# A perceiver block with a mixture of experts: down gather round eight PSUM banks, one loop over the down tiles, last down logits inside the first down steps

## Chip, core and metric

One core of one Trainium2 chip. The metric is the device time of one execution in microseconds (us), the median over several executions. Inputs and outputs are float32.

## The reference, cut to what matters

```python
x = x + cross_attention(layernorm(x), ctx)      # (32, 64, 512) queries, 1601 context rows each
x = x + causal_attention(layernorm(x))          # 16 heads
x = x + ffn(layernorm(x))

def kmoe(x_flat, W_router, A, B, scale, bias, d_in1, d_in2, d_out1, d_out2, top_k):
    logits = x_flat @ W_router.T                # 64 experts
    vals, idx = jax.lax.top_k(logits, 2)
    probs = jax.nn.softmax(vals, axis=-1)
    xs = x_flat.reshape(-1, d_in1, d_in2)
    Y = jnp.einsum('nkoi,nij,nkpj->nkop', A[idx], xs, B[idx])
    out = jnp.einsum('nkop,nk->nop', Y, probs)
    return out.reshape(-1, d_out1 * d_out2) * scale + bias

def ffn(x):                                     # rows of 1024: two tokens together, 1024 rows in all
    h = kmoe(x.reshape(-1, 1024), W_up, A_up, B_up, ..., 32, 32, 64, 64, 2)
    h = jax.nn.gelu(h, approximate=False)       # rows of 4096
    return kmoe(h, W_down, A_down, B_down, ..., 64, 64, 32, 32, 2)
```

## The kernel before

Everything that changes lies in `mixture`, the last of the stages: the feed-forward part with its two layers, "up" and "down". The 1024 rows are worked on in `T_N` = 4 tiles of 256 rows. Each engine runs its own block of instructions, and counting semaphores order them. VectorE (DVE), ScalarE (ACT), GpSimd (POOL) and SyncE (SP, which issues the DMAs) have straight code for all tiles; TensorE (`@block.tensor`) has loops on the chip (`pe.Fori`) and branches (`pe.If`), since its code is long: each float32 matmul of the program is recorded as two matmuls and two weight loads (a transpose as one of each).

A tile of the up layer on TensorE: `gather_up` in 8 rounds takes each row's factors out of the expert tables by a matmul with a one-hot matrix; `rows` transposes the next tile's rows; `logits_dn` forms the router logits of the down layer of the tile before (128 matmuls), `logits_up` those of the next tile, `fold_dn` adds two halves of the down logits; `steps_up` runs 16 steps in pairs: `first_up` twice (L1642), `second_up` twice (L1659). ScalarE copies the result of a first product out of PSUM (`mid_out`, L1515), stages input (`stage_x`), and applies gelu (`gelu`, L1520) to what VectorE wrote in `bias` (L1332). GpSimd stages the factors (`stage_a`, `stage_b`). In ScalarE's order each step n has: `mid_out(n)`, `stage_x(n+2)`, `gelu(n-2)`. The tile's hidden values go out to HBM by DMA.

After the last up tile come the down tiles. `gather_dn` (L1680) has two tables v = 0 and 1, and 8 units g in each; a unit is 8 matmuls (16 recorded) into two PSUM banks. Table 0 uses banks 0 to 3 and table 1 banks 4 to 7, so unit g waits until unit g-2 of its table has been copied out (`gather_out_dn`, VectorE L1342, ScalarE L1527). `BY_ACT` says which units ScalarE copies: 5 of the first 8 and 6 of the second. Then `steps_dn` runs 16 steps: `first_dn` (L1693, 32 matmuls, 64 recorded) into banks 0 to 3, `mid_out`, `second_dn` (L1708, 16 matmuls, 32 recorded) into bank 4 or 5, `y_out` (VectorE L1355). `steps_dn` is two first products, a loop of 7 rounds (second, first, second, first), and two second products. `stage_h` (VectorE, L1349), `stage_a_dn` (ScalarE, L1533) and `stage_b_dn` (GpSimd, L1215) feed it; `stage_b_dn` of step 0 waits for all evictions of table 1. `results_back` (VectorE transposes, L1362) and `residual` (L1368) finish a tile while the next is worked on. SyncE loads the hidden values of a tile (`load_h`, 4 transfers of 1 MB) and the residual input (`load_x2`, 2 of 512 KB).

What stands between: behind the first down gather TensorE runs the last tile's `logits_dn` (L1598) into banks 0 and 1, VectorE copies them out (`part`, L1449), TensorE folds them (L1605), VectorE copies the logits, and only then `steps_dn(0)` begins. `load_h(1)` waits for these logits. The choice of experts that they give (`greatest` to `weigh`) is made by VectorE beside the steps of down tile 0 and transposed behind them (`transpose_choices`, L1612). The loop over down tiles covers tiles 0 to 2, each with the gather of the next tile at its end; the last `steps_dn` stands after the loop as a second copy of the code:

```python
            gather_dn(0)
            all_units(pe, 0, 0)
            pe.wait_ge(s_gelu, T_N * STEPS)
            logits_dn()
            ...
            with pe.Fori(0, T_N - 1) as T:
                steps_dn(T)
                ...
                gather_dn(T + 1)
            steps_dn(T_N - 1)
```

Code of an engine comes from HBM by DMA. In the trace TensorE's arrives in pieces of 16 KB on the queue q8, the other engines' in pieces of 8 KB on q14.

## Time and profile before

| | us |
|---|---|
| median of 3 runs | 1546.29 |
| lowest, highest | 1537.84, 1546.94 |
| the profiled execution, its own time | 1545.56 |
| its span | 1543.6 |
| mean granted TensorE clock in it | 0.932 |
| TensorE busy (88% of the span) | 1363.7 |
| VectorE, ScalarE, GpSimd busy | 815.6, 443.3, 207.0 |

The profile is one execution. Times in its rows are microseconds from the start of the span, durations of one instruction nanoseconds. PE is TensorE's matmul side and PEld its weight loads, PEldq its sequencer. "Clock" is the share of TensorE's full clock of 2.4 GHz that was granted: 1.00, or 0.50, which is 1.2 GHz. "Issue" is time in which an engine waited for no other engine and no transfer that the profile knows.

### The profile page before, as it was taken

How to read it: one execution, taken by the hardware profiler on the slowest of the kernel's cores; microseconds unless marked ns; L12 is line 12 of the kernel's file. 1: busy time of each engine (PE TensorE's matmuls, PEld its weight loads, DVE VectorE, ACT ScalarE, POOL GpSimd, SP SyncE). 2: the span in 40 equal slices, each digit the busy share in tenths (PEclk: the TensorE clock that was granted, in tenths of full speed). 3: DMA queues.
4: the chain of work that ended last, by engine and by line, in shares of the span. 5: the costliest groups of instructions: out<-in, count | busy, mean ns of one | idle time of the engine just before them, and what ended most of it. 6: DMA issues, size and time to landing. Idle time of an engine off the chain costs nothing.

```text
span 1543.6 us, 70151 instructions
## 1 busy us (share of the span) xinstructions
PE 1363.7 (88%) x32072; PEld 931.8 (60%) x32072; DVE 815.6 (53%) x1511; ACT 443.3 (29%) x887; POOL 207.0 (13%) x361
## 2 busy tenths in 40 slices
PE   7896899999999999799999999867888888798887
PEld 4895454444444444366666666556677676677666
DVE  1224666566667665135655566443645645246645
ACT  0230211121112111122212122124544535336653
POOL 0000000000000000011111111113341432113211
PEclk9898899999999999999999999977999999769995
DMA  4575387687868885521111100130212206324102
GB/s 191 169 206 199 109 288 242 207 276 269 275 212 293 284 275 204 118 47 55 54 54 54 49 32 14 56 110 29 109 55 82 108 0 244 141 81 160 58 1 82
DMA packets 57230, 212.00 MB, mean 137 GB/s; under 512 B 11760, under 2 KB 28144, under 8 KB 42640
## 3 DMA queue, kind: packets, MB, share of 16 engines
q1 hardware_dynamic: 57104, 210.14, 39.8%
q8 instruction: 100, 1.64, 0.4%
q14 instruction: 26, 0.21, 0.0%
HBM read 172.37 MB, written 37.75 MB: 136 GB/s over the span
## 4 chain that ended last, share of the span: by engine, by line
PE 41%; DVE 5%; issue 5%; ACT 5%; POOL 2%; DMA 0%; DVEq 0%; POOLq 0%; SPq 0%; ACTq 0%
PE ps L895 8%; PE ps L1693 5%; PE ps L1627 4%; PE ps L886 4%; PE ps L996 4%; PE ps L1680 3%; PE ps L1642 2%; PE ps L1708 2%; PE ps L1598 2%; PE ps L916 2%; PE ps L1659 2%; ACT arena L1527 1%; PE ps L1589 1%; PE ps L906 1%; PE ps L938 1%
## 5 line engine op out<-in xcount | busy, mean ns | idle before, releaser
L476 DVE STREAM_TRANSPOSE arena<-arena 128x384 f32<-128x384 f32 (+1 forms) x512 | 276.7, 587 | 133.3 <-PE ps L563 132.4
L563 PE MATMUL ps<-arena 32*64 32x224 f32 (+3 forms) x8192 | 241.4, 348 | 28.4 <-issue 20.0
L563 PEld LDWEIGHTS ps<-arena 32*64 32x64 f32 x8192 | 160.5, 134 | 140.7 <-DVE arena L476 87.1
L587 PE MATMUL ps<-arena 128*64 128x512 f32 (+1 forms) x832 | 209.7, 615 | 0.1
L1515 ACT COPY arena<-ps 128x512 f32<-128x512 f32 x128 | 75.0, 586 | 167.6 <-PE ps L1642 86.2
L895 PE MATMUL ps<-arena 128*128 128x256 f32 x512 | 116.6, 387 | 6.3 <-ACT arena L847 6.3
L895 PEld LDWEIGHTS ps<-arena 128*128 128x128 f32 x512 | 97.3, 193 | 21.8 <-ACT arena L847 7.2
L534 ACT ACTIVATE arena<-ps,arena 128x416 f32<-128x416 f32 (+2 forms) x80 | 41.1, 531 | 229.9 <-DVE arena L488 229.9
L1693 PE MATMUL ps<-arena 64*64 64x32 f32 x4096 | 95.2, 250 | 10.0 <-issue 6.5
L587 PEld LDWEIGHTS ps<-arena 128*64 128x64 f32 (+1 forms) x832 | 49.5, 136 | 87.1 <-issue 87.1
L1693 PEld LDWEIGHTS ps<-arena 64*64 64x64 f32 x4096 | 88.7, 170 | 14.3 <-issue 10.9
L1332 DVE SCALAR_TENSOR_TENSOR arena<-ps,arena 128x512 f32<-128x512 f32 x64 | 69.3, 1110 | 49.0 <-PE ps L1659 49.0
L1627 PE MATMUL ps<-arena 64*32 64x128 f32 x4096 | 71.1, 277 | 14.9 <-issue 6.5
L1680 PE MATMUL ps<-arena 64*64 64x256 f32 x1024 | 70.0, 404 | 11.5 <-ACT arena L1527 5.0
L1627 PEld LDWEIGHTS ps<-arena 64*32 64x32 f32 x4096 | 59.5, 107 | 26.5 <-issue 22.7
L721 POOL MEMSET arena<- 128x128 f32 x1 | 0.2, 206 | 537.3 <-POOLq L432 537.3
L886 PE MATMUL ps<-arena 128*128 128x512 f32 x128 | 61.9, 620 | 8.2 <-ACT arena L876 4.8
L1642 PE MATMUL ps<-arena 32*32 32x64 f32 x4096 | 57.0, 233 | 13.4 <-issue 6.1
L1215 POOL COPY arena<-arena 128x512 f32<-128x512 f32 x64 | 40.9, 642 | 194.9 <-ACT arena L1527 99.6
L1680 PEld LDWEIGHTS ps<-arena 64*64 64x64 f32 x1024 | 42.8, 139 | 37.8 <-issue 30.9
L1642 PEld LDWEIGHTS ps<-arena 32*32 32x32 f32 x4096 | 47.9, 108 | 21.4 <-issue 21.0
L313 PE MATMUL ps<-arena 128*128 128x256 f32 x256 | 60.4, 395 | 0.0
(136 smaller groups left out, 1850.8 us busy)
## 6 DMA issues: line engine op xcount, KB each, us to landing
arena<-ctx SPq DMA_DIRECT2D x32, 1792.0 KB
arena<-ctx SPq DMA_DIRECT2D x32, 1280.0 KB
arena<-q_n SPq DMA_DIRECT2D x64, 256.0 KB, 13.9
h_n<-arena SPq DMA_DIRECT2D x16, 1024.0 KB, 4.5
arena<-h_n SPq DMA_DIRECT2D x16, 1024.0 KB, 8.3
arena<-x SPq DMA_DIRECT2D x16, 512.0 KB, 4.3
x_n<-arena SPq DMA_DIRECT2D x16, 512.0 KB, 3.1
arena<-x_n SPq DMA_DIRECT2D x16, 512.0 KB, 4.1
```

The costliest lines, as they stand in the source:

```text
L476: vec.transpose(z[:, at % RING, :, 0:nt * 32].rearrange("p b (j t) -> p b j t", t=32), slots[slot_of(k)][:, :, 0:nt, db * 32:(db + 1) * 32 ...
L563: last = pe.matmul(ps[b * SEQ:(b + 1) * SEQ, tb, g * 224:g * 224 + w], qs[p % 2][r, db, b * SEQ:(b + 1) * SEQ], z[r, at % RING, b, 0:w], s ...
L587: last = pe.matmul(ps[b * SEQ:(b + 1) * SEQ, OB, :], probt[0:r, j, b * SEQ:(b + 1) * SEQ], slot[0:r, b, jj, :], start=j == 0, stop=j == TI ...
L886: x = pe.matmul(ps[:, par, :], ats[:, c, par::2], w["xwv"][:, c, :], start=c == 0, stop=c == DC - 1)
L895: last = pe.matmul(ps[:, bank, m % 2 * QROWS:(m % 2 + 1) * QROWS], w[n][:, c, m * P:(m + 1) * P], lnt[:, c, :], start=c == 0, stop=c == DC ...
L996: last = pe.matmul(ps[:, 4 + par, :], aot[:, c, par::2], w["swo"][:, c, :], start=c == 0, stop=c == DC - 1)
L1332: vec.scalar_tensor_tensor(h[:, q, :, at].rearrange("p j g -> p g j"), ps[:, b:b + 2, :].rearrange("p b (g x) -> p (b g) x", x=2 * F1)[:, ...
L1515: act.copy(mid[u].rearrange("p (b x) -> p b x", b=2), ps[:, 2 * u:2 * u + 2, 0:256]).then_inc(s_me, 1)
L1627: last = pe.matmul(ps[c * R:(c + 1) * R, 4 * v + hf, o * P:(o + 1) * P], tab_st[v][r, o, :], x, start=True, stop=True)
L1642: last = pe.matmul(ps[q * R:(q + 1) * R, 2 * u + c // 2, m * F1:(m + 1) * F1], xs[rows_c, m, :], four(st_a[u])[rows_c, m // 2 * 2 + k, m % ...
L1680: last = pe.matmul(ps[t * E:(t + 1) * E, 4 * v + 2 * (g % 2) + hf, o % 2 * 2 * P:(o % 2 + 1) * 2 * P], tab_dn[v][r, o, :], x, start=True, ...
L1693: last = pe.matmul(ps[k * F1:(k + 1) * F1, 2 * u + t, g * D1:(g + 1) * D1], st_h[u][rows_t, g * F1:(g + 1) * F1], two(st_a[u])[rows_t, k, ...
```

## The change

- `gather_dn` goes round all eight banks: unit g of either table uses banks 2(g mod 4) and the next. A unit waits for the eviction of the fourth unit before it (`unit_out`), unit 2 of table 0 also for the last `y_out`; `steps_dn` waits for units 4 and 5 of table 1 before its two first products. `BY_ACT` gives ScalarE 4 and 5 units.
- The loop of TensorE over the down tiles covers all four; behind the last steps a branch skips the gather.
- `logits_dn` and `fold_dn` of the last tile move into rounds 0 and 2 of the step loop of tile 0, with banks 6 and 7, behind the branch `i < 3`; VectorE's copies and the choices move into steps 2 to 14. `exponential` on GpSimd moves from step 6 to 10, `next_choices` from 8 to 4.
- VectorE stages the first two steps and transposes results earlier in the gather.
- SyncE loads x2 of tile 0 after the logits. `y`, `yt` and `x2b` change places in SBUF.
- In the up layer ScalarE does the two `mid_out` and `stage_x` of a pair of steps, then its two gelus.

```diff
@@ -1025,8 +1025,8 @@
     wr_dn = wr_at.rearrange("p (o e) -> p o e", e=E)
-    y, yt = wr_at[:, 0:2 * D * 2].rearrange("p (t r b) -> p t r b", t=2, r=R), wr_at[:, 4 * D:8 * D].rearrange("p (t f) -> p t f", t=2)
-    x2b = tables["up_at"].rearrange("p (t f) -> p t f", t=2)
+    y = tables["up_at"].rearrange("p (t r b) -> p t r b", t=2, r=R)
+    x2b, yt = (wr_at[:, u * 4 * D:(u + 1) * 4 * D].rearrange("p (t f) -> p t f", t=2) for u in range(2))
     st_a, st_b, st_h = ([area(512) for _ in range(2)] for _ in range(3))
...
     hb_at = top_area.at
@@ -1055,7 +1055,7 @@
-    BY_ACT = ((0, 2, 4, 6, 7), (0, 2, 4, 5, 6, 7))
+    BY_ACT = ((0, 2, 4, 6), (0, 2, 4, 6, 7))
...
     s_wr, s_x2, s_end, s_hd = sem("mo_wr"), sem("mo_x2"), sem("mo_end"), sem("mo_hd")
@@ -1091,7 +1091,7 @@
         dst = fac[v].rearrange("p (m o f) -> p m o f", o=D1 // 2, f=2)[:, :, 2 * g:2 * g + 2, :]
-        b = 4 * v + 2 * (g % 2)
+        b = 2 * (g % 4)
         return dst, ps[:, b:b + 2, :].rearrange("p f (o m) -> p m o f", o=2)
...
     def unit_done(v, g, T):
@@ -1158,10 +1158,9 @@
                 load_h(0, q)
-            sp.wait_ge(s_ts, 16 * T_N)
-            load_x2(0)
             sp.wait_ge(s_hd, 16 * 4 * T_N)
             sp.wait_ge(s_lgd, T_N)
+            load_x2(0)
             for q in range(4):
...
             for T in range(T_N):
@@ -1245,19 +1244,23 @@
                     stage_b_dn(T, n)
-                    if T == 0 and n == 6:
+                    if T == 0 and n == 10:
                         exponential("dn", T_N - 1)
-                    if T + 1 < T_N and n == 8:
+                    if T + 1 < T_N and n == 4:
                         next_choices(T + 1)
...
         def _(vec):
-            def logits(k, i):
+            def parts(count, bank):
+                vec.wait_ge(s_lgd, count)
+                vec.tensor_copy(part, ps[:, bank:bank + 2, 0:P]).then_inc(s_part, 1)
+
+            def logits(k, i, bank):
                 if k == "up":
...
                     vec.wait_ge(s_lgb, i + 1)
-                vec.tensor_copy(lg[k], ps[:, 4 if k == "up" else 5, 0:2 * E].rearrange("p (t e) -> p t e", t=2)).then_inc(s_lge, 1)
+                vec.tensor_copy(lg[k], ps[:, bank, 0:2 * E].rearrange("p (t e) -> p t e", t=2)).then_inc(s_lge, 1)
...
                 vec.wait_ge(s_lge, choice(k, i)[1])
@@ -1375,7 +1378,7 @@
             vec.sem_inc(s_ohe["dn"][1], CREDIT)
-            logits("up", 0)
+            logits("up", 0, 4)
             greatest("up", 0)
...
             index("up", 0, 0)
@@ -1393,14 +1396,13 @@
                 if T:
-                    vec.wait_ge(s_lgd, T)
-                    vec.tensor_copy(part, ps[:, 0:2, 0:P]).then_inc(s_part, 1)
+                    parts(T, 0)
                 if T + 1 < T_N:
-                    logits("up", T + 1)
+                    logits("up", T + 1, 4)
                 else:
...
                 if T:
-                    logits("dn", T - 1)
+                    logits("dn", T - 1, 5)
                 for n in range(STEPS):
...
                     if T + 1 < T_N:
@@ -1442,16 +1444,11 @@
                             gather_out_dn(T, v, g)
-                        if v == 0 and g == 7 and T:
-                            results_back(T - 1, 0)
-                if T == 0:
-                    vec.wait_ge(s_lgd, T_N)
-                    vec.tensor_copy(part, ps[:, 0:2, 0:P]).then_inc(s_part, 1)
-                    logits("dn", T_N - 1)
-                stage_h(T, 0)
-                stage_h(T, 1)
-                if T:
-                    results_back(T - 1, 1)
+                        if v == 0 and g in (3, 7) and T:
+                            results_back(T - 1, g // 7)
+                        if v == 1 and g == 1:
+                            stage_h(T, 0)
+                            stage_h(T, 1)
                 for n in range(STEPS):
...
                         stage_h(T, n + 2)
@@ -1459,18 +1456,22 @@
                     if T == 0:
-                        if n == 1:
+                        if n == 2:
+                            parts(T_N, 6)
+                        if n == 6:
+                            logits("dn", T_N - 1, 6)
+                        if n == 7:
                             greatest("dn", T_N - 1)
                             difference("dn", T_N - 1)
-                        if n == 2:
+                        if n == 8:
                             index("dn", T_N - 1, 0)
...
                             index_out("dn", T_N - 1)
-                        if n == 4:
+                        if n == 9:
                             one_hot("dn", T_N - 1)
-                        if n == 10:
+                        if n == 13:
                             weights_of("dn", T_N - 1)
-                        if n == 11:
+                        if n == 14:
                             weigh("dn", T_N - 1)
...
                     one_hot_out("dn", T_N - 1, 7)
@@ -1546,12 +1547,14 @@
                     rows_out(T + 1)
-                for n in range(STEPS):
-                    mid_out(STEPS * T + n)
-                    if n + 2 < STEPS:
-                        stage_x(T, n + 2)
-                    if n >= 2:
-                        gelu(T, n - 2)
+                for n in range(0, STEPS, 2):
+                    for b in range(2):
+                        mid_out(STEPS * T + n + b)
+                        if n + 2 < STEPS:
+                            stage_x(T, n + b + 2)
+                    for b in range(2):
+                        if n >= 2:
+                            gelu(T, n + b - 2)
                 gelu(T, STEPS - 2)
...
                     one_hot_out("up", T + 1, 2)
@@ -1590,19 +1593,19 @@
-            def logits_dn():
+            def logits_dn(bank):
                 for p in range(F1):
...
                         half = p % 2
-                        last = pe.matmul(ps[half * E:(half + 1) * E, t, 0:P], wr_dn[r, p, :], h[r, :, p, :],
+                        last = pe.matmul(ps[half * E:(half + 1) * E, bank + t, 0:P], wr_dn[r, p, :], h[r, :, p, :],
                                          start=p < 2, stop=p >= F1 - 2)
...
-            def fold_dn(count):
+            def fold_dn(count, bank):
                 pe.wait_ge(s_part, count)
                 for t in range(2):
-                    last = pe.matmul(ps[:, 5, t * E:(t + 1) * E], part[:, t, :], fold, start=True, stop=True)
+                    last = pe.matmul(ps[:, bank, t * E:(t + 1) * E], part[:, t, :], fold, start=True, stop=True)
                 last.then_inc(s_lgb, 1)
...
             def transpose_choices(k, bank, count):
@@ -1661,23 +1664,28 @@
+            def unit_out(v, g, T):
+
+                done, first = unit_done(v, g, 0)
+                pe.wait_ge(done, T * (len(BY_ACT[v]) if g in BY_ACT[v] else 8 - len(BY_ACT[v])) + first)
+                apart(pe, SPARE)
+
...
                 for v in range(2):
-                    if v == 1:
-                        pe.wait_ge(s_ye, T * STEPS + CREDIT)
                     apart(pe, SPARE)
                     for g in range(8):
-                        if g >= 2:
-                            done, count = unit_done(v, g - 2, 0)
-                            pe.wait_ge(done, T * (len(BY_ACT[v]) if g - 2 in BY_ACT[v] else 8 - len(BY_ACT[v])) + count)
+                        if v == 0 and g == 2:
+                            pe.wait_ge(s_ye, T * STEPS + CREDIT)
                             apart(pe, SPARE)
+                        if v or g >= 4:
+                            unit_out(*divmod(8 * v + g - 4, 8), T)
                         for o in range(2 * g, 2 * g + 2):
...
                                     x = ohx_d[r, 0, 2 * t:2 * t + 2, :].rearrange("p k n -> p (k n)") if v == 0 else ohx_k[r, t]
-                                    last = pe.matmul(ps[t * E:(t + 1) * E, 4 * v + 2 * (g % 2) + hf, o % 2 * 2 * P:(o % 2 + 1) * 2 * P],
+                                    last = pe.matmul(ps[t * E:(t + 1) * E, 2 * (g % 4) + hf, o % 2 * 2 * P:(o % 2 + 1) * 2 * P],
                                                      tab_dn[v][r, o, :], x, start=True, stop=True)
@@ -1718,13 +1726,21 @@
             def steps_dn(T):
+                unit_out(1, 4, T)
                 first_dn(T * STEPS, 0)
+                unit_out(1, 5, T)
                 first_dn(T * STEPS + 1, 1)
...
                     first_dn(i * 2 + 3, 1)
+                    with pe.If(i < 3):
+                        with pe.If(i < 1):
+                            pe.wait_ge(s_gelu, T_N * STEPS)
+                            logits_dn(6)
+                        with pe.If(i > 1):
+                            fold_dn(T_N, 6)
                 second_dn(T * STEPS + STEPS - 2, 0)
@@ -1751,11 +1767,11 @@
                     apart(pe, SPARE)
-                    logits_dn()
+                    logits_dn(0)
                 with pe.If(T < T_N - 1):
...
                 with pe.If(T > 0):
-                    fold_dn(T)
+                    fold_dn(T, 5)
                 pe.wait_ge(s_lge, T * 2 + 2)
...
                 steps_up(T)
@@ -1768,21 +1784,16 @@
             gather_dn(0)
-            all_units(pe, 0, 0)
-            pe.wait_ge(s_gelu, T_N * STEPS)
-            logits_dn()
-            all_units(pe, 1, 0)
-            fold_dn(T_N)
-            pe.wait_ge(s_lge, 9)
-            with pe.Fori(0, T_N - 1) as T:
+            with pe.Fori(0, T_N) as T:
                 steps_dn(T)
                 with pe.If(T < 1):
+                    pe.wait_ge(s_lge, 9)
                     transpose_choices("dn", 6, T_N)
...
                         pe.wait_ge(s_ohe["dn"][e], 4 + CREDIT)
-                pe.wait_ge(s_oc, T * 2 + 2)
-                gather_dn(T + 1)
-            steps_dn(T_N - 1)
+                with pe.If(T < T_N - 1):
+                    pe.wait_ge(s_oc, T * 2 + 2)
+                    gather_dn(T + 1)
...
 _IN = ["x", "ctx", "wq", "wk", "bq", "bk", "bv", "xwv", "swq", "swk", "swv", "swo", "bo", "db",
```

## Rows read from the trace of the kernel before

**Rows 1.** The page, part 2: granted TensorE clock in 40 slices of the span.
```profile
PEclk9898899999999999999999999977999999769995
```

**Rows 2.** Windows: stretch, length, busy time (count) by engine, clock, DMA share, GB/s.
```profile
1296.00:1316.50 20.50, 17.43 (x256) 11.61 (x260) 6.12 (x5) 11.04 (x12) 0.00 (x0) 0.92 0.77 300
1316.50:1327.60 11.10, 8.55 (x267) 7.70 (x257) 1.43 (x4) 1.01 (x1) 1.17 (x2) 1.00 0.12 27
1327.60:1373.10 45.50, 38.44 (x1537) 36.11 (x1537) 17.84 (x43) 16.63 (x30) 11.21 (x17) 0.57 0.45 180
1376.10:1399.10 23.00, 20.98 (x384) 13.42 (x384) 11.85 (x10) 13.21 (x16) 1.11 (x2) 0.89 0.01 2
1399.10:1425.70 26.60, 22.89 (x1408) 20.98 (x1408) 17.14 (x30) 15.39 (x28) 10.74 (x17) 1.00 0.52 198
1425.70:1447.10 21.40, 18.71 (x389) 12.21 (x392) 12.13 (x11) 13.34 (x16) 1.22 (x2) 1.00 0.11 47
1447.10:1473.90 26.80, 22.98 (x1408) 21.21 (x1408) 17.04 (x31) 15.24 (x28) 10.77 (x17) 1.00 0.20 79
1473.90:1496.00 22.10, 18.51 (x384) 12.12 (x384) 12.11 (x11) 14.06 (x17) 1.50 (x2) 1.00 0.00 1
1496.00:1533.70 37.70, 34.67 (x1408) 32.20 (x1408) 17.33 (x30) 14.44 (x26) 8.62 (x14) 0.56 0.15 57
1376.10:1381.40 5.30, 5.25 (x52) 3.16 (x53) 1.22 (x1) 1.02 (x1) 0.00 (x0) 0.50 0.00 0
1118.40:1125.60 7.20, 7.20 (x257) 7.03 (x256) 0.00 (x0) 0.87 (x2) 0.00 (x0) 1.00 0.00 0
```

**Rows 3.** The chain that ended last, in tile 0's steps: start, us, what.
```profile
1330.73 3.91 issue
...
1338.34 2.60 issue
```

**Rows 4.** Timeline around the stalls of tile 0 and of the last tile.
```profile
1334.64 1.92 PE L1693 MATMUL ps<-arena 64*64 64x32 f32 x59 [3.91 <-issue]
...
1337.07 1.27 PE L1693 MATMUL ps<-arena 64*64 64x32 f32 x34
...
1499.98 0.26 PE L1708 MATMUL ps<-arena 128*32 128x32 f32 x4 [2.01 <-issue]
```

**Rows 5.** DMA queues: 1066 to 1296, 1397 to 1490, and 1490 to 1505 us.
```profile
q14 instruction: 4, 0.03, 0.0%
...
q14 instruction: 2, 0.02, 0.1%
...
q8 instruction: 3, 0.05, 1.4%
```

**Rows 6.** Branches of TensorE's sequencer: down step loop, and the `If` at L1751.
```profile
L1723 PEldq COMPARE_BRANCH  x28: 76/208/221, 1341.2 to 1531.6; - x28
...
L1751 PEldq COMPARE_BRANCH  x4: 74/78/3777, 1048.5 to 1253.5; - x4
```

**Rows 7.** Timeline: first product behind a loop return; three units without a wait.
```profile
1421.05 0.46 PE L1708 MATMUL ps<-arena 128*32 128x32 f32 x32 [0.33 <-issue]
...
1434.30 2.82 PE L1680 MATMUL ps<-arena 64*64 64x256 f32 x48 [0.37 <-DVE arena L1342]
```

**Rows 8.** Groups of instructions in the gather of tile 2, 1425.7 to 1444.6 us.
```profile
L1527 ACT COPY arena<-ps 128x1024 f32<-128x1024 f32 x10 | 10.1, 1032 | 8.5 <-PE ps L1680 8.5
...
L1342 DVE COPY arena<-ps 128x1024 f32<-128x1024 f32 x5 | 6.1, 1225 | 6.8 <-PE ps L1680 6.8
L1362 DVE STREAM_TRANSPOSE arena<-arena 128x1024 f32<-128x1024 f32 x2 | 4.3, 2164 | 0.0
```

**Rows 9.** Second product of the up layer: its waits for ScalarE; a pair's timeline.
```profile
  ACT arena L1515: 7.8, 20
...
1214.67 1.79 PE L1642 MATMUL ps<-arena 32*32 32x64 f32 x128 [0.24 <-issue]
...
1216.79 0.58 ACT L1515 COPY arena<-ps 128x512 f32<-128x512 f32 x1
```

## Prediction

> **What bounds the kernel now.** I read the page's clock strip first, then a table of stretches over the mixture's second half (the down layer), then the chain that ended last, then single instructions and instruction transfers. The strip shows TensorE at full clock except in a few places, the largest of them at slices 34 to 35 and at the end [rows 1]. The table says what they are [rows 2]. A down tile is a gather (16 units of 16 recorded matmuls) and 16 steps. From the second step product on, the steps take 26.8 us at granted clock 1.00 (tile 2), but 37.7 us at 0.56 in the last tile, with the same 1408 matmuls; tile 0, with 1537, takes 45.5 us at 0.57. So 0.5, the 1.2 GHz level, costs some 11 us per tile of steps. It comes after a stall of TensorE for "issue", that is for no other engine: 3.91 and 2.60 us in tile 0 [rows 3], 2.01 us in the last tile [rows 4]. Once lost there it is never regained inside the steps; in the gather of tile 1 it is regained after 5.3 us [rows 2].
>
> What stalls is code. Between the first stall and the second TensorE issued 59 more matmuls of one call, a second product (32), and 34 matmuls [rows 4]: (58.5 + 32 + 34) x 2, with a weight load for each matmul, and 7 waits make 256 instructions. Around the last stall three 16 KB instruction transfers run [rows 5]. The last `steps_dn` is a second copy of the code, run for the first time, so it pays for them; between 1397 and 1490 us, where the loop of tiles 1 and 2 repeats itself, there is not one such transfer on the queue of 16 KB pieces (q8), only the other one's, nor is there between 1066 and 1296, where the up loop goes round [rows 5].
>
> **Part by part.** The sum is for the profiled execution: 1545.6 us on its own clock, span 1543.6, 0.7 below the median of 1546.3.
>
> *Evictions ahead of gelu (up layer).* The second product of a pair starts when `mid_out` of the pair's second step ends. ScalarE now puts a gelu of 0.67 us ahead of that copy, so it begins at 1216.79 though its matmuls ended at 1214.67 + 1.79 = 1216.46 [rows 9]. TensorE waits for the copy 20 times, 7.8 us in all [rows 9]. Copy first, TensorE can start about 0.27 us sooner: 20 x 0.27 = 5 us. Bounds: 0, if GpSimd's staging, the other late one, ends as late; 8, all of the idle time. I take -5. The gelus themselves have room: ScalarE is not the bound of these steps.
>
> *Gather round eight banks.* Unblocked, a unit takes (2.82 - 1.09) / 2 = 0.87 us of TensorE [rows 7]; the evictions of a unit take 1.23 us on VectorE and 1.03 on ScalarE [rows 8]. With two pairs of banks per table each unit waits for the eviction two back, and from the first unit to the first second product pass 21.4 us [rows 2]. With four pairs it waits four back. The split becomes 9 units on ScalarE (9.3 us and two stagings) and 7 on VectorE: 7 x 1.23 + 2 transposes x 2.16 [rows 8] + 2 stagings x 0.55 = 14.0 us. I followed unit after unit: TensorE runs free until unit 8, then waits for VectorE, whose transposes delay units 5, 9 and 11; the 16th unit ends at 16.7 us, ScalarE's last eviction at 17.8, and the first second product can start at 18.8. Against 23.0, 21.4 and 22.1 us [rows 2] in tiles 1 to 3 (tile 1 starts its gather at half clock, which goes if tile 0 ends at full clock): -4.2, -2.6, -3.3, together -10. The added wait for `s_ye` before unit 2 is met before it comes. Bounds: 0 (eviction latency fills what the ring frees) to -13 (pure TensorE pace, 14.1 us).
>
> *Down logits inside step pair 0 of tile 0.* Today 11.1 us lie between gather and steps, 7.2 us of them the 256 recorded matmuls at their pace in the up layer [rows 2]. The matmuls stay; the 3 to 4 us of copying, folding and copying back go beside steps. Two more things follow. The transfers of the next hidden tile (4 MB, and now x2) wait for `s_lgd`, so they no longer collide with cold step code, where DMA held the fetch back and the stalls became 3.91 and 2.60 us; by then the loop's code has been run. And the logits are dense matmuls with 128 columns, like those (128 and 256 columns) under which the clock stays or comes back at 1.0 [rows 2]; I expect the clock, probably lost in the cold prelude, to come back there. Then: gather to 1313.5 (one cold block behind the hidden tile's load, 2 us), two first products at half clock with a stall 5.5, pair 0 at half clock 5.5, logits 10, six pairs at full clock 6 x 3.8 = 23, two second products 1: 1358.5, plus 0.4 because the weighing now sits at step 14. Today this point is 1373.1 [rows 2]. -14. Bounds: -4 (clock not regained: 12 steps at 2.45 instead of 1.75 us, logits 3 longer) to -18 (never lost).
>
> *One loop for all tiles.* If its code is resident, the last tile's steps run as tile 2's: 26.8 instead of 37.7, -10.9. Bounds: -11 and +1, below.
>
> *The branch in the step loop.* Each pair now ends in one more branch, taken in 21 pairs of tiles 1 to 3 (those of tile 0 are in the 3.8 above). A taken branch occupies the sequencer 0.21 us [rows 6] and the loop's own already shows as 0.33 us of idle TensorE [rows 7], so nothing hides the next. With the step behind it I take 0.3 us, +6.3. Bounds: 0 and 0.6 each, +13. At half clock the queue hides it.
>
> *The rest.* VectorE's chain of the last choices moves by one to six steps and ends in step 14; at 1.2 us of VectorE per step of 1.75 it fits. The load of x2 goes later by the same wait and is used from tile 1 on. `y` and `yt` change places only. Nothing: the cover is the slack of VectorE in the steps, without it about 1 us.
>
> Sum: -5 - 14 - 10 - 10.9 + 6.3 = -33.6; 1545.6 - 33.6 = 1512.
>
> **The rivals.** *A: the loop does not fit the code store (slower).* The down loop of today, counted from the calls, is 768 instructions of steps, 512 of gather, 16 of transposes and some 65 waits and register operations: 1362. It and the block behind it span 7 blocks of 256, and no trace row tests more. The new one has 512 more for the logits and two dozen waits: 1895, and from where it starts in its block it spans, with the one requested ahead, 9. If fewer than 9 are held, the head is gone at every return. A jump to absent code costs 3.78 us (the longest branch at L1751) [rows 6], of which about 3.4 show; this stands between gather and steps, so the steps run at half clock as in the last tile today. Each of tiles 1 to 3 then takes 18.8 + 3.4 + 36.7 (rows 2's 37.7 less the stall and the margin of its other waits) + 2.4 for the start of the gather = 61.3, less 2.4 in tile 1: 181.5 against 49.6 + 48.2 + 59.8 = 157.6 [rows 2], +24. With -5 and -14: 1550. If every block is fetched again, the block after the head (2.7) and the jump over the logits (3.3) come on top in each tile: 1568. It decides from the first tile return on. For it: the size. Against: nothing measured, the loops of today return freely. Middle 1560.
> The Trainium skill (Runtime: NRT & Kernel Launch, Instruction fetch mechanics) gives TensorE 128 KiB, 2048 instructions in blocks of 256: eight blocks, which speaks for A. The same section says that only two blocks are held and that a branch out of them stalls; the trace disagrees, the loop of 1362 goes back without a transfer [rows 5]. By the first A holds, by the second today's loops would stall in every tile.
> *B: only the head is fetched and the clock holds:* -33.6 + 3 x 3.4 = -23, 1522.
> *C: tile 0 does not regain the clock:* + 10, 1522. For it: 1327 to 1373 and 1496 to 1534, never regained in steps [rows 2]. Against: the gather regains it.
> *D: the ring and the branch cancel badly* (gather bound by eviction latency, 0; branches 0.6): -33.6 + 10 + 6.3, 1529. For it: waits of ScalarE's and VectorE's evictions on TensorE are long today, so they are not the bound; against.
>
> **How the numbers follow.** Forecast 0.38, A 0.36, B 0.08, C 0.12, D 0.06. Own range of the forecast 1503 to 1524. The range for the time reaches from there through A's lower and middle values, 1503 to 1566, and leaves out A's upper end and the bounds where all terms are best. About 1% (15 us) can be told from no change here. Faster by over 1% (below 1531): forecast, B, C, half of D and some of A, 0.58. Within 1%: the lower half of A, the rest of D, 0.23. Slower: A with every block fetched again, 0.19.
>
> **What would show it.** Right: in the table of stretches the granted clock is 1.00 in the steps of all tiles 1 to 3, each 28 to 29 us from the first second product; no q8 transfer after tile 0's gather of tile 1; gathers of about 16.5 us to the first step product with idle time before units released by VectorE; `COMPARE_BRANCH` twice per pair and about 0.3 us more idle before L1708's successor; pair 0 of tile 0 with logits, clock back to 1.00 at its end; fewer waits of the up layer's second product on the copy. Wrong: q8 transfers in each down tile and clock 0.5 behind each gather mean A. A time above 1531 without such transfers would mean that I misjudged the chain of VectorE in the gather or the branches.

## The result: slower, by code that the tile loop no longer holds

The changed kernel takes 1573.22 us (median of 4 runs, 1565.84 to 1576.85) against 1546.62 of the kernel before in the same runs: ratio 1.0175, 95% interval 1.0124 to 1.0226. The forecast was 1512, with a rival at 1568. The profiled execution is the shortest of the four, 1565.84 us, with a span of 1564.0.

The clock strip of the kernel after, to be held against [rows 1]:
```profile
PEclk8797999999999999899999999789999998957575
```
The last five slices (35 to 39, counted from 0; one is 39 us) hold the steps of the down tiles 1 to 3: three falls, one per tile. The table of stretches (columns as in [rows 2]): for each tile, from its first gather matmul to its first second product, and from there to its last one.
```profile
1284.10:1307.10 23.00, 18.52 (x388) 15.52 (x388) 10.39 (x10) 11.41 (x13) 1.17 (x2) 0.86 0.58 223
1307.10:1344.80 37.70, 33.52 (x1672) 31.32 (x1670) 16.92 (x43) 15.53 (x28) 11.26 (x17) 0.90 0.60 238
1347.20:1371.80 24.60, 18.81 (x388) 14.98 (x389) 13.87 (x12) 11.47 (x13) 1.17 (x2) 0.87 0.02 4
1371.80:1415.40 43.60, 36.68 (x1411) 34.08 (x1408) 17.28 (x30) 15.52 (x28) 10.09 (x16) 0.50 0.38 146
1415.50:1442.30 26.80, 21.04 (x384) 15.39 (x384) 14.08 (x13) 11.40 (x13) 1.17 (x2) 0.82 0.01 3
1442.30:1485.50 43.20, 36.72 (x1412) 34.11 (x1408) 17.27 (x30) 15.52 (x28) 10.08 (x16) 0.50 0.14 50
1485.60:1510.90 25.30, 20.18 (x388) 14.95 (x391) 14.05 (x13) 11.45 (x13) 1.17 (x2) 0.84 0.01 4
1510.90:1554.20 43.30, 36.64 (x1411) 34.08 (x1408) 17.29 (x30) 15.53 (x28) 8.58 (x14) 0.50 0.14 50
```
Tile 0 did what was hoped: its steps, logits included, run at a mean clock of 0.90 where they ran at 0.57 [rows 2]. Tiles 1 to 3 run all their steps at 0.50: 43.6, 43.2 and 43.3 us, against 26.6, 26.8 and 37.7 [rows 2]. From the start of its gather to the start of the next, or to its end, a tile took 49.6, 48.2 and 59.8 us and now takes 68.3, 70.1 and 68.6: 49 us more for the three.

The reason is told by the queues in the stretch of tile 2 (1415.5 to 1485.6 us), then by the branches of TensorE's sequencer (min/median/max ns; L1787 is the loop over tiles, L1738 the new `If` in the step loop):
```profile
q8 instruction: 9, 0.15, 1.0%
```
```profile
L1787 PEldq COMPARE_BRANCH  x4: 79/3587/3762, 1362.1 to 1557.6; - x4
L1738 PEldq COMPARE_BRANCH  x28: 75/218/4478, 1311.6 to 1551.8; - x28
```
Nine 16 KB transfers of code in a tile that had none [rows 5], and the return of the loop, 0.2 us where its code is at hand [rows 6], takes 3.76 us at 1362.1. The chain that ended last shows both places in every tile (start, us, what):
```profile
1364.13 2.52 issue
1384.12 3.81 issue
1434.68 2.51 issue
1454.37 3.63 issue
1503.85 2.17 issue
1522.92 3.85 issue
```
That is 2.2 to 2.5 us at the head, where the loop returns, and 3.6 to 3.9 where the first step pair jumps over the logits. The timeline of TensorE in tile 1's first pair shows the block's edge as well (start, us, line, count, idle before):
```profile
1366.65 1.50 PE L1701 MATMUL ps<-arena 64*64 64x32 f32 x47 [3.60 <-issue]
1369.19 2.65 PE L1701 MATMUL ps<-arena 64*64 64x32 f32 x81 [1.05 <-issue]
```
47 matmuls into the first product the code ends and TensorE waits 1.05 us for the next block.

### The profile page after: what moved, and what is told of

Same layout as the page of the kernel before. It is cut to its first block, busy times and chain, and to the rows that moved or that the text cites. A ratio compares the mean times of both kernels' runs of the same rounds, so it can differ in the third digit from the quotient of the medians.

```text
span 1564.0 us, 70207 instructions
## 1 busy us (share of the span) xinstructions
PE 1381.4 (88%) x32072; PEld 960.3 (61%) x32072; DVE 823.5 (53%) x1519; ACT 438.6 (28%) x879; POOL 204.9 (13%) x361
## 4 chain that ended last, share of the span: by engine, by line
PE 43%; issue 6%; DVE 5%; ACT 2%; POOL 2%; DMA 1%; SPq 0%; DVEq 0%; POOLq 0%; ACTq 0%
PE ps L895 7%; PE ps L1701 7%; PE ps L1630 4%; PE ps L886 4%; PE ps L996 4%; PE ps L1645 3%; PE ps L1716 2%; PE ps L1662 2%; PE ps L1601 2%; PE ps L916 2%; PE ps L1688 2%; PE ps L1592 1%; DMA arena<-h_n 1%; PE ps L906 1%; PE ps L938 1%
## 5 line engine op out<-in xcount | busy, mean ns | idle before, releaser
L1701 PE MATMUL ps<-arena 64*64 64x32 f32 x4096 | 117.2, 279 | 16.0 <-issue 15.7
L1701 PEld LDWEIGHTS ps<-arena 64*64 64x64 f32 x4096 | 108.5, 204 | 22.7 <-issue 18.7
L895 PE MATMUL ps<-arena 128*128 128x256 f32 x512 | 116.5, 386 | 6.2 <-ACT arena L847 6.2
L1335 DVE SCALAR_TENSOR_TENSOR arena<-ps,arena 128x512 f32<-128x512 f32 x64 | 68.6, 1104 | 42.4 <-PE ps L1662 42.1
L1630 PEld LDWEIGHTS ps<-arena 64*32 64x32 f32 x4096 | 59.5, 107 | 26.5 <-issue 23.0
L1358 DVE COPY arena<-ps 128x128 f32<-128x128 f32 x64 | 18.7, 292 | 103.3 <-PE ps L1716 103.1
L1688 PE MATMUL ps<-arena 64*64 64x256 f32 x1024 | 63.0, 399 | 10.0 <-DVE arena L1345 7.5
L1352 DVE COPY arena<-arena 128x512 f32<-128x512 f32 x64 | 51.1, 810 | 28.4 <-PE ps L1701 23.2
L1688 PEld LDWEIGHTS ps<-arena 64*64 64x64 f32 x1024 | 45.6, 141 | 25.9 <-issue 17.3
```

Source lines behind the costliest of these rows:

```text
L895: last = pe.matmul(ps[:, bank, m % 2 * QROWS:(m % 2 + 1) * QROWS], w[n][:, c, m * P:(m + 1) * P], lnt[:, c, :], start=c == 0, stop=c == DC ...
L1335: vec.scalar_tensor_tensor(h[:, q, :, at].rearrange("p j g -> p g j"), ps[:, b:b + 2, :].rearrange("p b (g x) -> p (b g) x", x=2 * F1)[:, ...
L1630: last = pe.matmul(ps[c * R:(c + 1) * R, 4 * v + hf, o * P:(o + 1) * P], tab_st[v][r, o, :], x, start=True, stop=True)
L1688: last = pe.matmul(ps[t * E:(t + 1) * E, 2 * (g % 4) + hf, o % 2 * 2 * P:(o % 2 + 1) * 2 * P], tab_dn[v][r, o, :], x, start=True, stop=True)
L1701: last = pe.matmul(ps[k * F1:(k + 1) * F1, 2 * u + t, g * D1:(g + 1) * D1], st_h[u][rows_t, g * F1:(g + 1) * F1], two(st_a[u])[rows_t, k, ...
```

## The experiments

Times are medians; ratios are against the kernel before, measured beside each kernel, with 95% intervals; its medians lay between 1543.6 and 1546.6 us. Stage lengths are from each kernel's own profile, which is one execution. The up stage repeats well: from the first up gather matmul to the first down one, all kernels without the new gelu order took 269.1 to 270.5 us and all with it 262.2 to 263.5. "Down stage" is from the first down gather matmul to the last second product: 237.5 us before, 269.9 after. The clock in the down stage repeats less well in the kernels whose code fits: the mean granted clock of a whole execution was 0.943 to 0.956 in four executions with two pair loops (the profiled one had 0.956) and 0.946 to 0.960 with the residual split (the profiled one had 0.946). So a profile that shows the clock falling or holding in a tile shows what happened once, not what happens each time.

**Spare code, first try (448 and 192 instructions, two kernels).**
```diff
+                with pe.If(T > 5):
+                    for _ in range(112):
+                        pe.matmul(...)
```


> The kernel before, with 112 matmuls (448 instructions) that are never executed behind a branch at the end of the loop over down tiles; nothing else changes. Theory S (the code store of TensorE holds 8 blocks of 256 instructions and is filled in order): the loop then spans 8 blocks and a ninth is requested ahead, so its head is gone at each return. Seven to eight q8 transfers in each of tiles 1 and 2, a COMPARE_BRANCH of about 3.8 us at the return, granted clock 0.5 in their steps, and some 40 us more in all (about 1588). Theory P (what slows the changed kernel is the order of its work, the branch per pair of steps or the wait for banks, and code is held whatever its size): no q8 transfer in tiles 1 and 2 beyond the first pass, one long branch at most, and 4 to 15 us more, all in tile 0 to 1.

Measured 1545.85 (1.0014, 0.9992 to 1.0035); with 48 matmuls 1541.43 (0.9996, 0.9973 to 1.0018). Neither tells anything about the size of code: T runs from 0 to 2, the condition was decided when the program was built, the spare code was left out of it, and the 16 KB transfers number 100 as before.

**Spare code that is really there.** In the kernel before, at the end of the loop over tiles:
```diff
+                with pe.If(T > 0):
+                    with pe.If(T < 1):
+                        for _ in range(112):     (second kernel: 48)
+                            pe.matmul(...)
```


> The kernel before with 112 matmuls (448 instructions) that no pass executes, at the end of the loop over down tiles, now behind two nested branches (first T > 0, then T < 1) that can't be decided when the kernel is built. Theory S (the code store holds 8 blocks of 256 instructions, filled in order): 9 blocks are wanted, so the loop's code is fetched again in tiles 1 and 2: seven to eight q8 transfers in each, a branch of about 3.8 us at the return and one over the skipped code, clock 0.5 in their steps, about 40 to 50 us more in all (1585 to 1595). Theory P (order, branch per pair and banks slow the changed kernel, not the size of its code): at most two long branches in the first pass, no q8 transfer in tiles 1 and 2, 4 to 15 us more.

> The same with 48 matmuls (192 instructions): 8 blocks with the one requested ahead. Theory S with a store of 8 blocks: no q8 transfer in tiles 1 and 2, clock 1.00 in their steps, the time of the kernel before within 3 us (two more branches a tile). A store of 7 blocks: as the run with 448. Theory P: as the kernel before.

Measured: 448 instructions 1599.01 us (1.0365, 1.0302 to 1.0427), 192 instructions 1546.04 us (1.001, 0.998 to 1.004). Neither block is ever executed. The stretches of tile 1 and tile 2's steps, first with 448:
```profile
1375.20:1409.70 34.50, 22.91 (x388) 15.05 (x388) 11.83 (x10) 13.14 (x15) 1.17 (x2) 0.75 0.02 4
1409.70:1447.30 37.60, 36.76 (x1414) 34.41 (x1412) 17.33 (x30) 15.54 (x28) 10.13 (x16) 0.50 0.45 168
1480.20:1518.10 37.90, 36.78 (x1413) 34.42 (x1412) 17.31 (x30) 15.55 (x28) 10.12 (x16) 0.50 0.15 57
```
and with 192:
```profile
1371.00:1392.70 21.70, 18.92 (x389) 12.18 (x389) 11.90 (x10) 13.21 (x16) 1.57 (x2) 1.00 0.01 3
1392.70:1419.50 26.80, 23.01 (x1408) 21.20 (x1408) 17.04 (x30) 15.49 (x28) 10.50 (x17) 1.00 0.50 201
```
The queues with 448, in a stretch of one tile (1400 to 1470 us):
```profile
q8 instruction: 7, 0.11, 0.7%
```
In the whole of tile 2, from its gather at 1447.3 to the next at 1518.1, there are 9. With 192 there is no transfer on that queue between 1391 and 1488 us. So nothing of the change but the mere length of the loop's code is needed: 1362 + 192 instructions (8 blocks of 256 with the one ahead) return freely, 1362 + 448 (9) fetch everything again, 53 us dearer. The branch of the loop's return takes 4.8 and 4.9 us with 448 and 0.2 with 192. The jump over the spare block costs as much as one over the logits: 3.34 to 3.69 us by its branches. This is rival A alone, in a kernel that has no other edit.

**The half-way house: logits ahead of the loop.** The change with the 512 instructions of the logits out of the step loop.
```diff
+            unit_out(1, 7, 0)
+            pe.wait_ge(s_gelu, T_N * STEPS)
+            logits_dn(6)
             with pe.Fori(0, T_N) as T:
...
-                        with pe.If(i < 1):
-                            pe.wait_ge(s_gelu, T_N * STEPS)
-                            logits_dn(6)
```


> The changed kernel with the 512 instructions of the down logits moved out of the step loop, ahead of the loop over down tiles; the ring of eight banks, the one loop, the branch per pair and all else stay. Theory S: the loop spans at most 8 blocks with the one ahead, so no q8 transfer after tile 0 and clock 1.00 in the steps of tiles 1 to 3, about 48 us a tile instead of 68 to 70; tile 0 loses its overlap and meets the hidden tile's load with cold code as in the kernel before. Together about 1521 to 1530, 1 to 2% faster than before. Theory P: the tiles stay at 65 us or more and the time above 1560.

Measured 1525.03 us (0.9882, 0.981 to 0.9954), 48 us below the change (45 by the ratios). No code is fetched after the first pass of the second gather. Yet the clock is at 0.5 from 1319.5 to 1367.3 in tile 0, and in tile 1 from 1394.6 to 1421.9, where nothing is fetched. TensorE's timeline there:
```profile
1391.96 0.46 PE L1716 MATMUL ps<-arena 128*32 128x32 f32 x32 [0.65 <-ACT arena L1516]
1393.02 1.16 PE L1701 MATMUL ps<-arena 64*64 64x32 f32 x64 [0.60 <-DVE arena L1352]
1394.13 0.46 PE L1716 MATMUL ps<-arena 128*32 128x32 f32 x32
1394.56 1.91 PE L1701 MATMUL ps<-arena 64*64 64x32 f32 x64
```
0.65 us behind the pair's branches (the profile names the copy on ScalarE that came last, but every pair at full clock has 0.64 or 0.65 there), then 0.60 us for VectorE's staging, held up by a residual addition of 1.45 us; two products later the same 64 matmuls take 1.91 instead of 1.14 us. Yet the same two gaps stand in tile 2, and there the clock stayed at 1.00:
```profile
1446.29 0.46 PE L1716 MATMUL ps<-arena 128*32 128x32 f32 x32 [0.64 <-ACT arena L1516]
1447.36 1.16 PE L1701 MATMUL ps<-arena 64*64 64x32 f32 x64 [0.61 <-DVE arena L1352]
```

**The parts alone, in the kernel before.** *Gelu order:*

> The kernel before with only ScalarE's order of the up layer changed (copies of a pair ahead of its gelus). My term: 20 waits of the second product for the copy go, 0.27 us each, so 5 to 6 us less, about 0.35%; the waits of L1659 for ScalarE fall from 7.8 us to under 1. If GpSimd's staging ends as late, nothing changes in time (0 to 2 us).

1538.07 us (0.9969, 0.9946 to 0.9993). The second product's waits for ScalarE, 7.8 us in 20 [rows 9], are now (us, times):
```profile
  ACT arena L1515: 0.5, 1
```
*A skipped branch per pair* (`with pe.If(i < 2): with pe.If(i > 1): pe.matmul(...)`, never run, in the step loop):

> The kernel before with one more branch (i < 2, never followed inside) at the end of each pair of down steps, over a single matmul that no pass executes. In tiles 1 and 2, at full clock, about 0.3 us more per pair: the stretch from the first second product on grows from 26.8 to about 29 us, idle before the pair's first L1708 from 0.33 to 0.65 us. At half clock nothing. 4 to 5 us in all if the clock stays at 1.00 in tiles 1 and 2; up to 20 more if these gaps next to VectorE's residual cost the clock there, as tile 1 of the run with the logits ahead suggests.

1547.29 us (1.0026, 0.9996 to 1.0057). Timeline at a loop return, where [rows 7] had 0.33:
```profile
1406.98 0.46 PE L1708 MATMUL ps<-arena 128*32 128x32 f32 x32 [0.60 <-issue]
```
0.27 us more at that gap; but the steps of tiles 1 and 2 take 27.7 us each against 26.6 and 26.8, 0.15 us per pair. The whole does not differ clearly from the kernel before. The clock did something here that the prediction's kernel did not show. It fell at 1329.8 behind a wait of 1.08 us for VectorE, and was back at 1.00 at 1333.2 after the two first products of tile 0, 128 matmuls of the steps' own shape without a gap:
```profile
1329.80:1333.20 3.40, 3.40 (x128) 3.40 (x128) 0.76 (x2) 1.11 (x2) 0.00 (x0) 0.50 1.00 424
```

*Ring of eight banks* (the lines of the diff for the gather's banks and waits, `BY_ACT` and VectorE's order):

> The kernel before with the gather round eight banks alone (split of the evictions, order of VectorE and the waits as in the change). Forecast's term: from first gather matmul to first second product 18.8 us in each of tiles 1 to 3 against 23.0, 21.4, 22.1, together -10 (1536). The code ahead of the step loop grows by some 10 instructions, 7 blocks stay, so nothing is fetched in tiles 1 and 2. Rival, eviction latency fills what the ring frees: 21 to 22 us, 0 (1546).

1530.15 us (0.9916, 0.9883 to 0.9949). Tiles 1 to 3 from gather to first second product:
```profile
1376.40:1396.10 19.70, 18.39 (x385) 13.27 (x387) 13.95 (x12) 11.48 (x14) 1.56 (x2) 0.93 0.01 2
1422.80:1441.00 18.20, 16.99 (x384) 13.21 (x384) 14.21 (x13) 11.48 (x14) 1.44 (x2) 1.00 0.10 40
1467.70:1487.30 19.60, 16.74 (x388) 13.44 (x389) 13.88 (x13) 12.43 (x15) 1.50 (x2) 1.00 0.01 1
```
*One loop alone* (`Fori(0, T_N)`, the wait for `s_oc` and the gather behind `If(T < T_N - 1)`, the last `steps_dn` gone):

> The kernel before with its last tile's steps taken into the loop over tiles (one copy of the step code, the gather of the next tile behind a branch), nothing else changed. The loop grows from 1362 by a few instructions, 7 blocks. Forecast's term: the last tile's steps at clock 1.00 in about 26.8 us instead of 37.7, -10.9, less a branch over the gather: 1533 to 1536. Rival, that the last tile pays in any loop (the jump over the gather's 512 instructions in the last pass meets absent code, or the clock is lost anyway): 0 to -4, 1540 to 1545.

1532.07 us (0.9909, 0.9877 to 0.9941). The last tile:
```profile
1476.30:1497.50 21.20, 18.63 (x384) 12.11 (x385) 11.87 (x11) 13.24 (x16) 1.16 (x2) 1.00 0.00 0
1497.50:1524.30 26.80, 23.03 (x1408) 21.26 (x1408) 16.98 (x30) 15.29 (x28) 9.34 (x15) 1.00 0.20 78
```
*The load of the next hidden tile held back* (`sp.wait_ge(s_ye, CREDIT + 8)` ahead of it):

> The kernel before, with the load of the next hidden tile held until y_out 8 of tile 0. It tells whether that 4 MB load is what made the two stalls of tile 0 (3.91 and 2.60 us) longer than those elsewhere. If it is: stalls of 2.0 to 2.5 us each, with the clock lost all the same, so the time falls by 2 to 3 us only (1542 to 1544, ratio about 0.998). Rival, the prediction's case of a clock never lost: with shorter stalls the clock holds in tile 0, -10 to -14 us (1533). Second rival, the load has nothing to do with it: stalls stay 3.9 and 2.6, time the same or up to 3 us longer, because stage_h of tile 1 waits for the later load.

1537.04 us (0.9964, 0.9939 to 0.9988). Where 3.91 us stood ahead of 59 matmuls [rows 4] there is now:
```profile
1328.55 1.92 PE L1694 MATMUL ps<-arena 64*64 64x32 f32 x59 [0.16 <-issue]
```
Tile 0 is 72.6 us from gather to gather against 80.1. And the stretch of the steps (1327.4 to 1364.3 us):
```profile
1327.40:1364.30 36.90, 36.34 (x1412) 34.21 (x1409) 16.98 (x41) 15.54 (x28) 11.19 (x17) 0.50 0.46 186
```
With the transfers of code undisturbed, cold step code costs almost nothing at half clock. The second stall, 2.60 us, stood at half clock in the kernel before too, and is gone, so it was the load's doing. The first began at full clock there and meets half clock here, so the load accounts for a part of its 3.91 us only: at full clock, with nothing else on the queues, such a block still cost 1.77 and 1.75 us in the small loop below. Neither the expected 2.0 to 2.5 us nor the unchanged 3.9 came. The clock fell at 1326.15, ahead of these steps, and all of them ran at 0.50. What stood ahead of the fall are waits for VectorE of 0.62 us (of the fold) and then:
```profile
1324.70 2.75 PE L1694 MATMUL ps<-arena 64*64 64x32 f32 x128 [1.08 <-DVE arena L1350]
```
The prediction's "It comes after a stall of TensorE for issue" is thus not the whole of it. Nor do these waits decide it: the kernel before has them as well and held the clock until the stall of 3.91 us.

**Small loop.** Ring, gelu order and one loop, with the first products behind the gather, the logits between tile 0's first products and the loop, the fold behind tile 0's steps, the last choices in tile 1, no branch in the step loop, the next load after `y_out` 6.

> A version of the changed kernel that keeps its ring, its one loop and its order in the up layer, but not the size and the branch: the two first products of a tile stand behind the gather, the last down logits between those of tile 0 and the loop (no copies needed before the steps go on), the fold behind the steps of tile 0, the choices in tile 1, no branch in the loop of pairs, x2 and the next hidden tile loaded after step 6 of tile 0. Theory S: loop about 1380 instructions, no q8 transfer after the gather in tile 0, clock 1.00 in the steps of tiles 1 to 3, 46 us a tile; tile 0 at half clock behind its cold code (or at full, if stalls of 1 us leave the clock). 1500 if it stays, 1512 if not; in any case under 1525 and the fastest so far. Theory P (the ring and the moved logits cost time themselves): not faster than before.

1522.79 us (0.9869, 0.982 to 0.9918), above the 1500 to 1512 that were expected. Tiles 2 and 3 are as they should be (steps 26.8 and 26.5 us at 1.00), tile 0's steps ran at 0.59, and tile 1's at 0.50 (36.4 us), behind a last cold block, fetched at 1375.1 on queues that moved nothing else:
```profile
1378.62 0.65 PE L1718 MATMUL ps<-arena 128*32 128x32 f32 x32 [1.75 <-issue]
```

**Half of the logits ahead.** The change, with 256 instructions of the logits ahead of the loop and 256 inside: some 1640 in the loop.
```diff
+            logits_dn(6, 0, F1 // 2)
             with pe.Fori(0, T_N) as T:
...
-                            logits_dn(6)
+                            logits_dn(6, F1 // 2)
```


> The changed kernel with the first half of the down logits (256 instructions) ahead of the loop over tiles and only the second half inside the first step pair. The loop falls from 1895 to some 1640 instructions, which span 7 blocks of 256, 8 with the one requested ahead. Theory (store of 8 blocks): no transfer of code in tiles 2 and 3, none at the return; tile 0 gets its clock back behind the half of the logits inside; the time comes near what was forecast for the change: 1512 to 1522 (ratio 0.98), the upper end if the extra branches and VectorE's residual cost the clock in tile 1 as they did with the logits ahead. Rival, that it is the jump over the logits or the loop's form and not the size that costs: 9 transfers in a tile or the clock lost behind each gather as in the change, 1560 to 1573.

1515.32 us (0.982, 0.9791 to 0.985): 58 us below the change (55 by the ratios), from moving 256 instructions. This is the forecast's design, with its code at hand; the last transfer of code is at 1367.9. One tile of steps still lost the clock without a fetch:
```profile
1433.66 0.46 PE L1717 MATMUL ps<-arena 128*32 128x32 f32 x32 [0.65 <-ACT arena L1516]
1434.72 1.86 PE L1702 MATMUL ps<-arena 64*64 64x32 f32 x64 [0.60 <-DVE arena L1352]
```
The same pair of gaps as with the logits ahead, in tile 2 this time. Tile 1 has it as well and kept the clock:
```profile
1386.92 0.46 PE L1717 MATMUL ps<-arena 128*32 128x32 f32 x32 [0.65 <-ACT arena L1516]
1387.98 1.16 PE L1702 MATMUL ps<-arena 64*64 64x32 f32 x64 [0.61 <-DVE arena L1352]
```
So over the two kernels this pair of gaps stood four times and the clock fell behind two of them.

**The residual split.** That kernel, with VectorE's two residual additions of a tile (behind steps 3 and 5) made four of half the columns:
```diff
-                    if T and n in (3, 5):
-                        residual(T - 1, n // 5)
+                    if T and n in (3, 5, 7, 9):
+                        residual(T - 1, n // 6, n // 2 % 2 ^ 1)
```


> The kernel with half of the logits ahead, and VectorE's residual additions of a tile (two of 1024 columns, 1.46 us each, behind steps 3 and 5) split in four of 512 columns behind steps 3, 5, 7 and 9. In the unsplit kernel TensorE waited 0.65 us (branch) and then 0.60 us for the staging behind the residual in tile 2, and the clock fell to 0.5 for 30.7 us. Theory, that pair of gaps costs the clock: the wait for staging goes to 0 to 0.2 us, the clock stays 1.0 in tiles 1 to 3, tile 2's period falls from 53.8 to 46.5 us: -6 us, about 1509. Rival, the clock falls in some tile for another reason: a 0.5 stretch of 25 to 35 us in one tile again, 1515.

1506.0 us (0.9727, 0.9682 to 0.9771). Tile 2 from its first second product:
```profile
1427.50:1454.70 27.20, 22.69 (x1408) 20.87 (x1408) 17.83 (x32) 15.48 (x28) 10.59 (x17) 1.00 0.20 77
```
27.2, 27.2 and 27.1 us in tiles 1 to 3, all at 1.00. The wait for staging is gone and the clock holds, and the ratio is lower by 0.009, with intervals that do not meet. That fits the theory of the two gaps, but the profile shows one execution, and half of these pairs did no harm unsplit: how often the split saves the clock is not shown. In the profiled execution, the longest of the four, what remains is tile 0, which fell to 0.5 at 1333.6 behind this gap:
```profile
1331.48 0.46 PE L1721 MATMUL ps<-arena 128*32 128x32 f32 x32 [1.11 <-ACT arena L1520]
```

**Two pair loops round one copy of the code**, without and with the residual split: the steps in loops of 1 and 6 pairs inside an outer loop of two, the second half of the logits between them, the rest as in the small loop.

> As the one with half of the logits ahead, but the step pairs of a tile run in two loops of 1 and 6 pairs round one copy of the code (an outer loop of two), the second half of the logits stands between them, the fold behind the steps of tile 0 and the choices in tile 1: 2 more branches in a tile instead of 7. Theory: 8 blocks, clock 1.0 in tiles 1 to 3 and in tile 0 from its second pair on; -5 us against the one with half ahead from the branches, 1505 to 1515. If the clock is lost in tile 1 all the same, it is the waits for VectorE's residuals and not the branches, + 8 us: 1515 to 1523.

> The kernel with two pair loops round one copy of the code, with the residual additions split in four. There the clock was already 1.0 in tiles 1 to 3; the waits for staging behind the residuals are 1.3 us per tile in tiles 1 to 3. Theory: only those waits go, -2 to -4 us, 1505. Rival: VectorE's two additional instructions and the later end of the additions give it back, 1508.

1508.54 us (0.9797, 0.9765 to 0.983) and 1506.77 us (0.9728, 0.9674 to 0.9782). The profiled execution of the first, its shortest, kept 1.00 in all steps; its tiles are not shorter, 28.8, 28.3 and 28.0 us, since the outer loop costs a gap of its own. With the split, tiles 1 and 2 take 28.4 and 27.4 us, and tile 3 lost the clock behind that gap (34.9 us); by the medians nothing can be told between the two kernels:
```profile
1468.68 0.46 PE L1723 MATMUL ps<-arena 128*32 128x32 f32 x32 [1.22 <-ACT arena L1522]
```
But both kernels have this gap in each of tiles 1, 2 and 3, 1.21 to 1.22 us, and the clock held over the other five. Tile 2 of the unsplit and of the split kernel:
```profile
1420.34 0.46 PE L1719 MATMUL ps<-arena 128*32 128x32 f32 x32 [1.21 <-ACT arena L1518]
1422.17 0.46 PE L1723 MATMUL ps<-arena 128*32 128x32 f32 x32 [1.21 <-ACT arena L1522]
```
A gap of this size alone made the fall the exception.

**Fold behind tile 0.** Half of the logits ahead, residuals split, one branch per pair, the fold and the choices as in the small loop.

> Half of the logits ahead, half behind the first step pair through one branch, the residual additions split in four, the fold behind the steps of tile 0 and the choices' chain of VectorE in tile 1. No gap inside a tile's steps over 0.65 us is left but the code stalls of tile 0's first pass. Theory (gaps of over 1.1 us cost the clock): 1.0 in all of tiles 1 to 3 and in tile 0 from its second pair on; tile 0 is some 8 us shorter than in the kernel with half ahead and the residual split: 1498 to 1502. Rival: the clock is lost somewhere all the same, in a stretch of 30 to 45 us: 1506 to 1512.

1503.74 us (0.9743, 0.9705 to 0.9781), 2.6% below the kernel before and 69 us below the change (67 by the ratios). That lies between the 1498 to 1502 of the theory and the 1506 to 1512 of its rival. Steps of tiles 0 to 3:
```profile
1312.70:1346.30 33.60, 28.48 (x1537) 26.13 (x1538) 14.98 (x29) 15.51 (x28) 10.46 (x16) 0.95 0.49 195
...
1368.30:1396.40 28.10, 22.74 (x1408) 20.64 (x1408) 19.92 (x45) 15.44 (x28) 11.46 (x17) 1.00 0.27 102
...
1419.00:1446.20 27.20, 22.69 (x1408) 20.92 (x1408) 17.79 (x32) 15.52 (x28) 10.61 (x17) 1.00 0.20 77
...
1465.30:1492.40 27.10, 22.69 (x1408) 20.87 (x1408) 17.39 (x32) 15.46 (x28) 8.68 (x15) 1.00 0.20 77
```
Tile 0 is 58.7 us from gather to gather against 73.0 with the fold inside. Not all of that is the clock: the load is later too, and this kernel moves the choices. The down stage is 202.7 us, of 237.5 before. The whole cannot be told from the 1506.0 with the residual split by these runs.

## Why the prediction was wrong

The step that failed is *One loop for all tiles*, -10.9 us, whose sum began "If its code is resident": it was not. In place of steps of 26.8 us at 1.00 the runs showed 9 transfers of code in every pass, a return of 3.4 to 3.8 us, a jump over the logits of 3.6 to 3.9 us and steps of 43.2 to 43.6 us at 0.50: tiles 1 to 3 took 207 us where they had taken 157.6. Everything behind it (steps at 1.00 in tiles 1 to 3, the branch and ring terms at full clock) hung on that condition. The right case was written down as rival A, with the right count (9 blocks) and place, but given 0.36, and its full form was left outside the range. "Against: nothing measured, the loops of today return freely" was weak evidence: today's loops span 7 blocks with the one ahead and say nothing of 9. The chances were also added up wrongly: forecast, B, C and half of D alone make 0.61 for a time below 1531, not 0.58, and D's sum is 1528, not 1529; neither bears on the cause.

Point by point:

- *Gelu order*, -5 (0 to -8). Up stage 269.7 to 263.3 us in the change, 262.4 alone; -7 by stages, -5 by the ratio. Right; the waits for ScalarE fell from 20 to 1, not by a share, so the stage's figure lies near the upper bound.
- *Ring*, -10 in tiles 1 to 3. Alone 19.7, 18.2 and 19.6 us against 23.0, 21.4 and 22.1: -9.0. The working of 18.8 was near. Not in the sum: tile 0, 72.8 us against 80.1, its gather shorter and its stalls of code with it, 2.82 and 2.50 instead of 3.91 and 2.60. Whole: 0.9916, 13 us.
- *Tile 0 with the logits inside*, -14. To the end of tile 0: 60.7 us against 77.1, -16.4. The clock was regained under the logits, at 1314.3, as expected. Part of it is tile 0's share of the ring (7.3 us alone), so the gain of the logits' place by itself is smaller; it was not run alone.
- *One loop*, -10.9. Alone, in a loop that fits: last tile 59.8 to 48.0 us, -11.8; ratio 0.9909. The term was right under its condition.
- *Branch per pair*, +6.3. Alone 0.15 us per pair at full clock, +3.2 for 21 pairs: the term was twice too large, since a pair grew by less than the 0.27 us of its gap. What the branch may cost beside its time is the clock, which was no term at all: with 0.65 us in place of 0.33 ahead of the wait for VectorE's staging, the clock fell in two of four cases, and in none where 0.33 us stood there. That is case C's idea in another place, tiles 1 and 2 instead of 0.
- *Rival A, full form.* Gather and steps of a tile 61.3 + 2.7 + 3.3 = 67.3 us (64.9 in tile 1); measured 68.3, 70.1 and 68.6. Its 1568 stands against 1565.84 in the profiled execution and a median of 1573.22. The jump over the logits was priced at 3.3 and showed as 3.6 to 3.9, the head at 3.4 and showed as 2.2 to 2.5 in the chain (3.3 to 3.6 us of idle TensorE), the block behind it at 2.7 and showed as 0.8 to 1.05. What was missing are the steps, taken from a tile with a clock of 0.56 and run at 0.50. So the sum came near in part because its errors cancel.
- The Trainium skill (Runtime: NRT & Kernel Launch, Instruction fetch mechanics) gives TensorE's store 2048 instructions in blocks of 256, which makes eight. The runs with 192 and 448 skipped instructions agree with it: 8 blocks, counting the one requested ahead, go round freely (1546.04 us), 9 do not (1599.01). The same section of the Trainium skill says that two blocks are held, with 32 KiB beside it, the size that it gives for most other engines. For TensorE no run bears that out: with 192 nothing is fetched for 97 us, the length of two tiles.

With its code at hand the forecast's design takes 1515.3 us, and 1506.0 once the residual is split as well; the forecast was 1512.0 with an own range of 1503 to 1524. The mechanisms were read rightly; whether the loop still fits was not.

Open: what exactly makes the clock fall in a tile of steps. It fell behind long code stalls. Behind gaps of 0.65 and 0.60 us in a row it fell in two of four cases, behind 1.21 to 1.22 us in one of six, behind 1.11 us once; it held over 1.06 us in tile 0 of the change, over 1.01 us in tile 0 with half of the logits ahead, over 0.41 and 0.80 us in a row, and over 0.33 and 0.53 to 0.60 us in a row each time. So the length of the last gap does not decide it; no run tested what does.

## What to carry to other kernels

Count the instructions of a loop with everything in its body, also what runs in one pass only: a skipped block takes its place in the store and turns a free return into a fetch of the whole loop. If a case hangs on such a size, give it more than an even chance when the count passes anything that the trace has shown to work, or put blocks that run once outside, in part if need be: 256 instructions moved were worth 58 us. Where losing the clock costs a tile of steps 7 to 11 us, a gap of a microsecond may cost far more than its length, though it need not: give it a chance, and look at more than one execution before calling it the cause. Spreading long operations of the engine that feeds TensorE is a cheap guard.

## What was not expected of the hardware

- From free to full fetch it is one block. Loops of 1554 and some 1640 instructions return without a fetch, loops of 1810 and 1895 fetch 9 blocks in every pass; no run lies between. One block too many (448 instead of 192 spare instructions) cost 53 us over tiles 1 to 3. A store that gives up its oldest block for each new one would do this; the runs show the effect, not the rule of replacement.
- What a cold block costs depends on what stands beside it. Entered straight on at half clock it cost 0.16 us with quiet queues and 2.60 us beside a 4 MB load; at full clock up to 2.0 us with quiet queues (1.22 with the fold behind tile 0, 1.77 and 1.75 in the small loop, 2.01 in the last tile of the kernel before) and 3.91 us beside the load. The branch of a jump to one lasted 3.3 to 4.9 us.
- The steps never regained 1.00 in 43 us (tiles 1 to 3 of the change); the logits inside tile 0's steps brought it back, and the steps behind them kept it. The shape of the matmuls alone does not decide it: with the branch alone, 128 step matmuls without a gap brought it back as well (1329.8 to 1333.2 us).
- A second jump in a pair costs little time (0.15 us). But with a gap of 0.65 us in place of 0.33, ahead of a wait of 0.60 us for another engine, a tile lost its clock in two of four cases, 7 us each.
